# Adding the experts' sums by accumulating DMA loads, with the last down projections moved ahead of four mixings

## The reference, cut to what matters

```
attention:  Y = (A * Q) @ W_out + b_out + xn        # A: one row per sequence, from sums over all its tokens
experts:    y      = scatter_add over 16 experts of  w * (silu(xg @ w_gate) * (xg @ w_up)) @ w_down
            shared = silu(xn @ sw_gate) * (xn @ sw_up) @ sw_down
out = x + attention + (y + shared)
```

## Time and profile before

| | us |
|---|---|
| median of three runs | 174.53 (173.79 to 174.89) |
| the profiled execution | 175.58 |
| its span, first to last instruction | 173.8 |

### The profile page before, as it was taken

How to read it: one execution, slowest core, us unless ns; L and a number is a source line. 1 busy time by engine, 2 the same in 40 slices (tenths; PEclk the granted TensorE clock), 3 DMA queues, 4 the chain that set the end, 5 groups by cost and what they waited for, 6 DMA issues and landing times.

```text
span 173.8 us, 3137 instructions
## 1 busy us (share of the span) xinstructions
PE 154.6 (89%) x1005; PEld 136.0 (78%) x1005; DVE 110.9 (64%) x321; ACT 74.9 (43%) x227; POOL 98.8 (57%) x126
## 2 busy tenths in 40 slices
PE   7977897997699699999699979999999999999950
PEld 6556776996597478998478868997899888899950
DVE  1887798586447348479985686866845434374590
ACT  3034336685148988454554444526522335410000
POOL 8674599408626305599856894587444333330691
PEclk9997899999879999999999999999999999999998
DMA  5999979490101721756547656566367222226967
GB/s 156 342 375 339 542 240 335 152 274 9 23 9 39 237 94 28 168 160 162 161 70 182 160 160 122 135 160 175 66 177 190 31 30 34 30 30 177 305 230 258
DMA packets 25507, 28.53 MB, mean 164 GB/s; under 512 B 4114, under 2 KB 24563, under 8 KB 25460
## 3 DMA queue, kind: packets, MB, share of 16 engines
q1 hardware_dynamic: 21042, 22.90, 41.9%
q0 software_dynamic: 3072, 4.33, 14.7%
q10 hardware_dynamic: 1378, 1.12, 2.0%
HBM read 21.64 MB, written 8.79 MB: 175 GB/s over the span
## 4 chain that ended last, share of the span: by engine, by line
DMA 33%; PE 23%; POOL 14%; issue 9%; ACT 9%; DVE 8%; POOLq 1%; DVEq 0%; ACTq 0%; SPq 0%
DMA ysum<-eo,idx 28%; PE bank L245 5%; PE bank L1173 5%; PE bank L247 4%; PE bank L246 4%; POOL xn_all L462 3%; DMA x_all<-ysum 3%; DMA xg<-rows,idx 2%; DVE st L670 2%; ACT xt_all L493 2%; POOL zsum L402 1%; DVE xt_all L700 1%; ACT junk L523 1%; PE bank L1035 1%; PE bank L1086 1%
## 5 line engine op out<-in xcount | busy, mean ns | idle before, releaser
L431 POOL DMA_INDIRECT ysum<-eo,idx x16 | 29.3, 1830 | 27.5 <-DMA ysum<-eo,idx 24.5
L245 PE MATMUL bank<-wkvr_s,xt_all 128*128 128x256 f32 (+1 forms) x96 | 30.5, 317 | 5.3 <-DVE xt_all L700 3.1
L246 PE MATMUL bank<-wkvr_s,xt_all 128*128 128x256 f32 (+1 forms) x96 | 28.2, 294 | 0.0
L247 PE MATMUL bank<-wkvr_s,xt_all 128*128 128x256 f32 (+1 forms) x96 | 28.2, 294 | 0.0
L423 POOL DMA_INDIRECT xg<-rows,idx x16 | 20.3, 1269 | 11.1 <-DVE idx L848 4.1
L1173 PE MATMUL bank<-xgt,wgu 128*128 128x128 f32 (+1 forms) x192 | 24.0, 275 | 1.3 <-ACT xgt L588 1.3
L245 PEld LDWEIGHTS bank<-wkvr_s,xt_all 128*128 128x128 f32 x96 | 19.2, 200 | 6.9 <-DVE xt_all L700 4.1
L1173 PEld LDWEIGHTS bank<-xgt,wgu 128*128 128x128 f32 (+1 forms) x192 | 22.4, 187 | 1.7 <-issue 1.7
L245 PE MATMUL bank<-xt_all,sw_s 128*128 128x512 f32 (+1 forms) x48 | 20.8, 433 | 0.0
L246 PEld LDWEIGHTS bank<-wkvr_s,xt_all 128*128 128x128 f32 x96 | 19.2, 200 | 0.0
L247 PEld LDWEIGHTS bank<-wkvr_s,xt_all 128*128 128x128 f32 x96 | 19.2, 200 | 0.0
(11 more groups left out here) (167 smaller groups left out, 358.9 us busy)
## 6 DMA issues: line engine op xcount, KB each, us to landing
wgu<-in_w_gu SPq DMA_DIRECT2D x16, 368.0 KB, 3.3
rows<-xn_all SPq DMA_DIRECT2D x4, 512.0 KB, 6.5
wdn<-in_w_dn SPq DMA_DIRECT2D x16, 128.0 KB, 3.6
x_all<-ysum SPq DMA_DIRECT2D x4, 512.0 KB, 6.4
x_all<-in_x SPq DMA_DIRECT2D x3, 512.0 KB, 6.5
trg<-in_trig SPq DMA_DIRECT2D x1, 1024.0 KB, 5.8
out<-xn_all ACTq DMA_DIRECT2D x4, 256.0 KB, 2.7
out<-xn_all SPq DMA_DIRECT2D x4, 256.0 KB, 2.6
```

The lines of the kernel that those rows point to most:

```text
L245: nc.tensor.matmul(dst, lt_hi, r_hi, start=start, stop=False)
L246: nc.tensor.matmul(dst, lt_hi, r_lo, start=False, stop=False)
L247: return nc.tensor.matmul(dst, lt_lo, r_hi, start=False, stop=stop)
L431: nc.gpsimd.indirect_dma_start(out=ysum, out_offset=bass.IndirectOffsetOnAxis(ap=idx[:, e:e + 1], axis=0), in_=eo[:, e % G, :], in_offset= ...
```

## The change

SyncE no longer loads `ysum`. GpSimd, once it has seen the sixteenth scatter land, issues four DMAs, one for each group, in the order 2, 0, 3, 1, that read `ysum` from DRAM and add it into `sh` in SBUF as they land (`accum_op`). The additions of GpSimd and VectorE and the buffer `yin` are gone. A group's DMA waits until the group's shared part is in (`kept`), and for groups 0 and 1 also until the mixings of the group are done (`half_done`); for groups 2 and 3 the mixings wait for the DMA. On TensorE and VectorE, `unit(16)`, `unit(17)` and their two `keep`s stand ahead of the mixings of tiles 4 to 7 instead of behind them.

```diff
@@ sync
-            sp.wait_ge(acc_done, TILES)
-            sp.wait_ge(scat_done, 16 * E)
-            for g in (2, 3, 0, 1):
-                sp.dma_start(yin[:, g * G:(g + 1) * G, :], ysum_v[:, g * G:(g + 1) * G, :]).then_inc(y_in[g], 16)
 
             for t in range(0, 2 * G, 2):
-                sp.wait_ge(ot_dve, min(t + 2, 5))
-                if t >= G:
-                    sp.wait_ge(ot_pool, (9, 11)[t // 2 - 2])
+                sp.wait_ge(half_done, t + 2)
+                sp.wait_ge(y_in[t // G], 16)
                 sp.dma_start(out_v[:, t:t + 2, :], sh[:, t:t + 2, :]).then_inc(out_sent[t // 2], 16)
@@ gpsimd
-            def add_y(t):
-                pool.wait_ge(y_in[t // G], 16)
-                nc.gpsimd.tensor_tensor(sh[:, t, :], sh[:, t, :], yin[:, t, :], ALU.add).then_inc(ot_pool, 1)
...
+            def add_y(g):
+
+                pool.wait_ge(kept, 2 * g + 2)
+                if g < 2:
+                    pool.wait_ge(half_done, G * g + G)
+                nc.gpsimd.dma_start(sh[:, g * G:(g + 1) * G, :], ysum_v[:, g * G:(g + 1) * G, :], accum_op=ALU.add).then_inc(y_in[g], 16)
+
+            pool.wait_ge(scat_done, 16 * E)
+            for g in (2, 0, 3, 1):
+                add_y(g)
@@ vector
                 if t >= 2 * G:
-                    dve.wait_ge(ot_pool, t - 2 * G + 1)
+                    dve.wait_ge(y_in[t // G], 16)
...
-            for t in range(1, 2 * G):
+            for t in range(1, G):
                 mix(t)
             keep(16)
             keep(17)
-            for t in range(2 * G, 3 * G):
+            for t in range(G, TILES):
                 mix(t)
-            add_y(0)
-            mix(3 * G)
...
@@ tensor
-            for t in range(2 * G):
+            for t in range(G):
                 if t == 1:
                     pe.wait_ge(mid_done, 2 * E)
                 mixed(t)
@@ tensor
             unit(17)
-            for t in range(2 * G, TILES):
+            for t in range(G, TILES):
```

More of the change, by code:

```diff
@@ L125, in layer @@
         x_all = sb("x_all", [P, TILES, D])
-        k_all = yin = x_all
+        k_all = x_all
         xn_all = sb("xn_all", [P, TILES, XW])
@@ L219, in layer @@
             sem(n) for n in ("red_done", "cs_done", "comb_done", "acol_done", "aw_done", "m_done", "m_hi", "m_lo"))
-        s2_done, att_done, half_done, ot_pool, ot_dve = (
-            sem(n) for n in ("s2_done", "att_done", "half_done", "ot_pool", "ot_dve"))
+        s2_done, att_done, half_done = (
+            sem(n) for n in ("s2_done", "att_done", "half_done"))
         y_in, out_sent = sems("y_in", GROUPS), sems("out_sent", 2 * GROUPS)
@@ L458, in _ @@
             scatter(E - 1)
-            def add_y(t):
-                pool.wait_ge(y_in[t // G], 16)
-                nc.gpsimd.tensor_tensor(sh[:, t, :], sh[:, t, :], yin[:, t, :], ALU.add).then_inc(ot_pool, 1)
-            pool.wait_ge(kept, 6)
-            for t in range(2 * G, 3 * G):
[L466 to L472, removed]
+            def add_y(g):
[6 more added lines that the diff above has]
+                add_y(g)
         @block.scalar
```

## The result

The changed kernel takes 179.27 us (median of four runs, 178.12 to 179.64), the kernel before 174.71 in the same set of runs: 1.0246 times as long, with an interval of 1.0167 to 1.0326. It is slower by 4.6 us; the forecast was 181.0 with 73% on slower.

What follows compares the result with a forecast made beforehand. Scatters set the tail's start at 156.7 us; 3.2 writing, 0.3 start, four transfers at 3.4, 2.1 for results, then landing and last results end the span 6.5 us later: 174.53 + 6.5 = 181.0, own range 178 to 185.

Steps and rivals of the forecast that it cites:

- Writing and start: Tail, GpSimd: writing the first accumulating DMA takes 3.2 us, and its transfer starts 0.3 us later.
- The rate: Tail, DMA engines: accumulating rows move at 154 GB/s, 3.4 us a group, 13.6 us for four.
- Rival B: Accumulating rows in the tail cost twice plain ones, 2.86 us a group; 2.7 us slower, 177.2; chance 0.22.
- What follows the accumulating rows: Tail's end: 2.1 us for results sharing the engines, 0.4 to landing, 3.4 for SyncE's last results, 0.6 to span end.
- The swap at nothing: TensorE, down units ahead of mixings 4 to 7: same sum, mixing 8 starts where it did, cost nothing.
- rival D: Reorder in the tail does not act if GpSimd's writing takes over 1.6 us a DMA; changes no time; no chance given.
- Rival A: Addition in the tail's loads is free, 1.43 us a group; 2.3 us faster, 172.2; chance 0.20.
- C's 5.0 us a group: Accumulating rows in the tail cost what the scatter's did, 156 ns each; 12.9 us slower, 187.4; rival C's chance 0.18.
- Its floor of 171.5: Span end set by TensorE's last mixing, VectorE's mix, 2.7 us to landing and 0.6; at most 2.3 us gained.
- The estimate of 3.2 us from issue to landing: Tail: a 512 KB load issued by GpSimd lands 3.2 us after issue, group 1 at 165.8.
- the marks that the prediction set: Signs in the changed profile: GpSimd's writing times, queue cost per KB, VectorE's and SyncE's waits, TensorE idle before its last mixings.
- The down units: Sign on TensorE: if the moved down units don't start near 154.7 us, the swap has a missed cost.

Runs made afterwards that it cites:

- swap_only: The kernel before with only the order changed, units 16 and 17 and their keeps ahead of mixings 4 to 7; 175.27 us, ratio 1.0043.
- sp_loads_no_add: The changed kernel with SyncE's four plain loads in place of GpSimd's DMAs and no addition at all; 174.22 us, 0.9979 of the kernel before.
- acc_4k: The changed kernel accumulating into the free token buffer's straight rows, source read in 4 KB pieces; 179.42 us, 1.0257 times the kernel before.

## Why the prediction was right

The direction, the place and the mechanism held: the scatters' edge was left alone, GpSimd's and VectorE's additions cost little on the path, and an accumulating row is dearer than a plain one. The measured 4.6 us stand against 6.5 forecast, and the own range of the forecast, 178 to 185, held 179.3. By the terms of its sum, for the tail (forecast 3.5 + 13.6 + 6.5 = 23.6, measured 21.3):

- **Writing and start, 3.5 us forecast, 3.6 measured, right by luck.** GpSimd writes a DMA every 1.33 us (single records, which overlap, of 1.25 to 2.28), not every 3.2; the gather and scatter rows of 128 rows were nearly the price of 512. But the rows then start slowly: 67 GB/s from 158 to 160, as if the full stream had begun at about 160.1, with 0.13 MB moved. Two errors of some 2 us cancelled.
- **The rate, 13.6 us forecast, 10.0 measured (1.97 MB at 197 GB/s).** This is the term that was mis-sized. The price of a row in the records was read rightly: 106 ns in the scatter's best slice, 102 in the full stream (a share of 1.23 at 197 GB/s). The error is the step from there to a rate. It scaled 139 GB/s at a share of 0.90 up to a share of 1.0 and called that full, though the plain loads stand at 1.09 in rows 7; the accumulating stream ran at 1.23, so a row passes every 83 ns and not every 106. At 1.23 the same slice gives 190 GB/s, close to what was measured. Rival B's 2.86 us a group came nearest to the 2.7 of the runs, by way of the plain row times two.
- **What follows the accumulating rows, 6.5 us forecast (2.1 for shared results, 0.4, 3.4 and 0.6), 7.7 measured (170.1 to 177.8).** The prediction let half of three groups' results slip in beside the rows. They didn't: up to 168.8 us 0.01 MB had, and nearly the whole 2 MB left afterwards. Rival B's rate in the forecast's sum, 3.5 + 11.4 + 6.5 = 21.4, meets the measured tail of 21.3, but by errors that cancel: B's 11.4 is 1.4 too long for what was left after the slow start, and the end 1.2 too short.
- **The swap at nothing (and rival D): right**, shown by swap_only, though for another reason than given. GpSimd was not too slow to use it; group 3's DMA did go before 159.96. The engines' backlog made it worthless: at that time two groups were still to be moved.
- **Rival A and its floor.** A is refuted by 195 against 373 GB/s, and C's 5.0 us a group by the 2.7 measured. Its floor of 171.5, TensorE's last mixing plus one result transfer, was too low by 1.1 us of tail: sp_loads_no_add shows that the results come as a burst and take 3.3 to 4.8 us. By its time there was nothing to gain that shows, and by the lower end of its interval 0.7%, about 1.2 us, not 2.3. The estimate of 3.2 us from issue to landing, worked out from the Trainium skill, "DMA: Bandwidth & Descriptors" (Anatomy of one DMA), for one DMA by itself, is too short here, where several are out at a time: 6.8 to 12.8 for accumulating loads, and 4.5 at the least for plain ones of GpSimd.

Of the marks that the prediction set, one failed: TensorE did not stand idle before its last mixings. It worked through them without a gap and was done by 165.7, 3 us ahead of group 3's landing, so its results waited for VectorE in the banks. The down units started at 152.6 and not near 154.7, with TensorE 2 us ahead from before the swap on, so that mark says nothing against the swap. The rest held in kind: VectorE waited for group 2 until 163.4 (forecast 164) and for group 3 until 168.9 (171), SyncE for group 1 until 173.9 (176). GpSimd's queue shows 102 ns of engine time per KB in the records as forecast, but shares above 1 mean that the records of an engine overlap, so the rate by GB/s is the one to use.

What stays open: why the first 2 us of rows run at a third of the rate (acc_4k, whose DMAs are written in 0.85 to 1.25 us, moves 188 GB/s from 3 us behind its first issue on, where the changed kernel moves 174 from 3.5 us on; that half microsecond may be the writing and doesn't settle it), and why the last rows of a GpSimd DMA come so thinly that group 1 lands more than 3 us behind the bulk. Neither was tried alone.

## What to carry to other kernels

An addition made by the DMA engines is not free: here it cost them 1.9 times the plain transfer. So count bytes against what else must pass in the same stretch, here 2 MB of results. Before replacing engine work in a tail, ask what it is hidden behind: with all additions removed this kernel was no faster. And mind the queues: transfers written far ahead on GpSimd's queue held back those that were issued later on another. Read shares of the DMA engines against the highest that the same view shows for a full stream (1.09 plain, 1.23 accumulating), not against 1.

## What the runs showed that was not expected

- A result transfer issued behind three written groups took 7.9 us to land, and 2.4 us when the queue was short, although the two are on different queues.
- GpSimd's plain load of rows of 1 KB went in packets of 4 KB and took 0.75 to 0.84 us to write; with the addition each row was a packet and it took 1.25 to 2.28 us. With sources of 4 KB in one piece it was 0.85 to 1.25.
- Straight or crooked rows in SBUF made no difference to the accumulating rate (193 and 195 GB/s).
